# Zero-padded patch matrices for the depthwise convolutions, and layer norms cut into four slices

## The reference, cut to what matters

```
x = mamba_layer(x)                                    # layer 0, a selective scan
g = group_norm(x)                                     # layer 1
x = x + conv1x1(concat(dw3(g), dw5(g), dw7(g))) + b   # three depthwise convolutions
t = tokens(x)                                         # 4 x 4096 tokens of 96 values
for layer in (2, 3):
    t = t + linear_attention(ln(t))                   # no softmax: q (k^T v), 6 heads
    t = t + mlp(ln(t))                                # 96 -> 384 -> 96, values in fp8 e5m2
out = image(t)
ln(v) = (v - mean(v)) / sqrt(var(v) + 1e-5)           # over the 96 values of a token
```

## Time and profile before

| | us |
|---|---|
| median of 3 runs | 4298.84 (4298.52 to 4301.72) |
| the profiled execution, its own time | 4304.14 |
| its span | 4302.3 |
| PE busy | 3678.2 (85%) |
| DVE busy | 3358.8 (78%) |
| POOL busy | 2847.3 (66%) |
| ACT busy | 2386.9 (55%) |
| mean granted clock of TensorE | 0.88 |

### The profile page before, as it was taken

One profiled execution on the slowest core, in us unless ns is written; L12 is line 12 of the kernel. 1 busy time (PEld: TensorE's weight loads), 2 busy tenths in 40 slices (PEclk: granted clock), 3 DMA queues, 4 the chain that ended last, 5 costly groups with the idle time before them and its releaser, 6 DMA issues. The chain is left out here.

```text
span 4302.3 us, 38111 instructions
## 1 busy us (share of the span) xinstructions
PE 3678.2 (85%) x10080; PEld 1484.1 (34%) x10080; DVE 3358.8 (78%) x3987; ACT 2386.9 (55%) x4025; POOL 2847.3 (66%) x2326
## 2 busy tenths in 40 slices
PE   6999899999999999999999999998349987585666
PEld 2333333333333333333333333332113325363554
DVE  4999999999999999999999999999710005646565
ACT  5667666667666666766666766665221112424335
POOL 4988999998899998899998889998300000303113
PEclk8999999999999999999999999999755557676666
DMA  2655555556555565555455555455765564100001
GB/s 86 175 158 161 159 168 156 160 174 166 156 169 156 161 171 159 160 155 161 157 161 163 160 152 165 150 156 159 169 169 163 163 159 110 30 15 15 15 1 30
DMA packets 281726, 588.59 MB, mean 137 GB/s; under 512 B 65847, under 2 KB 135098, under 8 KB 280358
## 3 DMA queue, kind: packets, MB, share of 16 engines
q1 hardware_dynamic: 214438, 516.93, 40.8%
q10 hardware_dynamic: 67072, 69.23, 6.2%
HBM read 532.16 MB, written 58.28 MB: 137 GB/s over the span
## 5 line engine op out<-in xcount | busy, mean ns | idle before, releaser
L796 POOL TENSOR_TENSOR prod<-states,c_rows 128x512 f32<-128x512 f32 x1536 | 1920.4, 1270 | 182.6 <-DVE states L726 148.9
L726 DVE TENSOR_TENSOR_SCAN states<-decay,carry,bpsum 128x512 f32<-128x512 f32 x1344 | 1676.7, 1259 | 0.0
L455 PE MATMUL ypsum<-prod,identity 128*128 128x512 f32 x3072 | 1599.8, 604 | 0.5 <-POOL prod L796 0.3
L561 ACT ACTIVATE decay<-delta,decay_rate 128x512 f32<-128x512 f32 x1344 | 934.7, 711 | 312.1 <-DVE states L726 307.7
L706 DVE TENSOR_TENSOR bpsum<-bpsum,dx 128x512 f32<-128x512 f32 x1344 | 904.4, 673 | 139.8 <-PE bpsum L448 125.4
L1641 POOL TENSOR_TENSOR y<-y,b 128x384 f16<-128x384 f16 x64 | 60.9, 951 | 1054.4 <-ACT y L1458 1054.3
L455 PEld LDWEIGHTS ypsum<-prod,identity 128*128 128x128 f32 x3072 | 583.7, 194 | 433.1 <-issue 285.9
L448 PE MATMUL bpsum<-b_rows,select 96*128 96x512 bf16 x1344 | 521.9, 389 | 209.7 <-DVE states L726 206.4
L448 PEld LDWEIGHTS bpsum<-b_rows,select 96*128 96x128 bf16 x1344 | 129.8, 97 | 960.6 <-DVE states L726 670.6
L1048 PE MATMUL convp<-image,patch_w 88*96 88x512 f32 x384 | 328.0, 1057 | 44.4 <-DMA image<-normed_map 44.4
L561 ACT ACTIVATE bpsum<-delta,decay_rate 128x512 f32<-128x512 f32 x192 | 132.6, 691 | 309.3 <-DVE states L726 308.5
(11 more groups left out here) (188 smaller groups left out, 4538.3 us busy)
## 6 DMA issues: line engine op xcount, KB each, us to landing
c_rows<-bc_map SPq DMA_DIRECT2D x512, 512.0 KB, 3.8
c_rows<-bc_map SPq DMA_DIRECT2D x512, 256.0 KB, 4.0
b_wide<-bc_map ACTq DMA_DIRECT2D x128, 256.0 KB, 4.5
image<-normed_map SPq DMA_DIRECT2D x192, 96.1 KB
depthwise_map<-dw_sums ACTq DMA_DIRECT2D x96, 192.0 KB, 2.7
dw_parts<-depthwise_map SPq DMA_DIRECT2D x16, 1152.0 KB, 7.5
b_wide<-bc_map ACTq DMA_DIRECT2D x128, 128.0 KB, 4.3
normed_map<-padded SPq DMA_DIRECT2D x8, 1155.0 KB, 13.8
```

Source lines behind the costliest of these rows:

```text
L455: pe.matmul(ypsum[:, group % Y_BANKS, :], identity[:, :], prod[:, n % P_RING, :], start=s == 0, stop=s == STATES - 1).then_inc(summed, 1)
L561: act.activation(into, delta[k % 2][:, g, :], ACT.Exp, scale=decay_rate[:, ORDER[k][0], g, s:s + 1]).then_inc(done, 1)
L726: dve.tensor_tensor_scan(states[:, n % H_RING, :], by, add, carry[:, at, u:u + 1], ALU.mult, ALU.add).then_inc(scanned, 1)
L796: pool.tensor_tensor(prod[:, n % P_RING, :], states[:, n % H_RING, :], c_rows[:, n // C_STATES % C_RING, n % C_STATES, :], ALU.mult).then_ ...
```

## The change

It does two things.

The tiles `patch_w` and `image` are made 128 partitions tall, and a patch matrix 128 columns wide. POOL clears both whole before the first load, behind its memsets of `padded`; `zeroed` now comes after the last, and SP waits for it ahead of the first patch loads. The loads go into rows 0 to 87 and columns 0 to 95. Each matmul is of 128 inputs and 128 outputs into all of the bank; ACT still copies 96 rows out. A patch load now has elements of 96 floats (384 bytes), 8 to a partition, where one element had 3072 bytes.

The layer norms are cut into four slices of 8 tiles. Every step takes a slice number k, and its semaphores count slices. In attention DVE makes the four slices of center, add_input where due, the four of variance, the Gram steps, and then one slice of scale after each of the additions 1, 3, 5 and 7; ACT makes one slice of squares after each of the copies 1, 3, 5 and 7, and the four of roots at the end. In MLP the steps of slice k come after the chunks k (center), k + 1 (squares), k + 2 (variance), k + 3 (roots) and k + 4 (scale). Ahead of phase 0 the slices stand between the `add_input`s. A slice of center waits only for its own quarter of the residual, and PE waits before the transposes of a chunk for the slice that it reads.

```diff
-SQUARE_AFTER, ROOT_AFTER = (5, 3), 5
-CENTER_AFTER, VARIANCE_AFTER, SCALE_AFTER = 1, 4, 6
+SLICES = 4
+ATT_SQUARE, ATT_SCALE = (1, 3, 5, 7), (1, 3, 5, 7)
+MLP_CENTER, MLP_SQUARE, MLP_VARIANCE, MLP_ROOT, MLP_SCALE = range(5)
...
-            patch_w = tmp("patch_w", [PATCH, W_RING, W_CHANNELS, 2, PATCH_OUT])
-            image = tmp("image", [PATCH, I_RING, BATCH * ROW_BLOCKS, HALF_ROW])
+            patch_w = tmp("patch_w", [128, W_RING, W_CHANNELS, 2, 128])
+            image = tmp("image", [128, I_RING, BATCH * ROW_BLOCKS, HALF_ROW])
...
-                        sp.dma_start(patch_w[:, j % W_RING, :, :, :].rearrange("p c t m -> p (c t m)"),
+                        sp.dma_start(patch_w[0:PATCH, j % W_RING, :, :, 0:PATCH_OUT].rearrange("p c t m -> p (c t) m"),
                                      dram["patch_rows"][:, W_CHANNELS * j:W_CHANNELS * (j + 1), :, :]
-                                     .rearrange("p c t m -> p (c t m)")).then_inc(patch_loaded[j % W_RING], 16)
+                                     .rearrange("p c t m -> p (c t) m")).then_inc(patch_loaded[j % W_RING], 16)
...
+                    sp.wait_ge(zeroed, 1)
                     for j in range(W_RING):
                         load_patches(j)
...
-                            last = pe.matmul(banks[0:PATCH_OUT, c % 4, :].rearrange("m (n i) -> m n i", i=HALF_SIDE),
+                            last = pe.matmul(banks[:, c % 4, :].rearrange("m (n i) -> m n i", i=HALF_SIDE),
...
                     for i in range(2):
-                        last = pool.memset(padded[:, i, :, :, :, :].rearrange("c f r n i -> c (f r n i)"), 0.0)
-                    last.then_inc(zeroed, 1)
+                        pool.memset(padded[:, i, :, :, :, :].rearrange("c f r n i -> c (f r n i)"), 0.0)
+                    pool.memset(patch_w[:, :, :, :, :].rearrange("p j c t m -> p (j c t m)"), 0.0)
+                    pool.memset(image[:, :, :, :].rearrange("p c n i -> p (c n i)"), 0.0).then_inc(zeroed, 1)
...
                 def turn(p, c, kind, rows):
 
                     fill = fills[kind, p, c]
+                    pe.wait_ge(ln_ready, SLICES * p + c * SLICES // CHUNKS + 1)
...
-                def squares(v):
-
-                    act.wait_ge(ln_centered, v + 1)
-                    act.activation(haug[:, v % 2, :, 0:C], dev[:, :, :], ACT.Square).then_inc(ln_squared, 1)
+                def squares(v, k):
+
+                    act.wait_ge(ln_centered, SLICES * v + k + 1)
+                    tiles = slice(SLICE * k, SLICE * (k + 1))
+                    act.activation(haug[:, v % 2, tiles, 0:C], dev[:, tiles, :], ACT.Square).then_inc(ln_squared, 1)
...
-                        if p + 1 < PHASES and c == SQUARE_AFTER[0]:
-                            squares(p + 1)
+                        if p + 1 < PHASES:
+                            for k in due(ATT_SQUARE, c):
+                                squares(p + 1, k)
                     if p + 1 < PHASES:
-                        roots(p + 1)
+                        for k in range(SLICES):
+                            roots(p + 1, k)
...
                     if layer == 0 and not is_mlp:
-                        dve.wait_ge(rows_taken, CONV_GROUPS * (b + 1))
+                        dve.wait_ge(rows_taken, CONV_GROUPS * b + k + 1)
                     elif not is_mlp:
-                        dve.wait_ge(t_step, CHUNKS * (nth(v - 2) + 1))
+                        dve.wait_ge(t_step, CHUNKS * nth(v - 2) + CHUNKS // SLICES * (k + 1))
                     else:
-                        dve.wait_ge(t_taken, fills[ATT_O, v - 2, CHUNKS - 1] + 1)
+                        dve.wait_ge(t_taken, fills[ATT_O, v - 2, CHUNKS // SLICES * (k + 1) - 1] + 1)
...
                     dve.tensor_tensor(gram[:, 0, 0:C], mp[0:C + 1, 0, 0:C], bff[:, layer, :], ALU.add).then_inc(gram_step, 1)
-                    if p + 1 < PHASES:
-                        scale(p + 1)
...
                                           src[:, tiles, :].rearrange("p j c -> p (j c)"), ALU.add).then_inc(t_taken, 1)
+                        if p + 1 < PHASES:
+                            for k in due(ATT_SCALE, c):
+                                scale(p + 1, k)
...
-                            if c == CENTER_AFTER:
-                                center(p + 1)
-                            if c == VARIANCE_AFTER:
-                                variance(p + 1)
-                            if c == SCALE_AFTER:
-                                scale(p + 1)
+                            if 0 <= c - MLP_CENTER < SLICES:
+                                center(p + 1, c - MLP_CENTER)
+                            if 0 <= c - MLP_VARIANCE < SLICES:
+                                variance(p + 1, c - MLP_VARIANCE)
+                            if 0 <= c - MLP_SCALE < SLICES:
+                                scale(p + 1, c - MLP_SCALE)
...
-                for i in range(CONV_GROUPS):
-                    add_input(i)
-                center(0)
-                add_input(CONV_GROUPS)
-                variance(0)
-                add_input(CONV_GROUPS + 1)
-                scale(0)
-                for i in range(CONV_GROUPS + 2, 2 * CONV_GROUPS):
-                    add_input(i)
+                for i in range(2 * CONV_GROUPS + 1):
+                    if i < 2 * CONV_GROUPS:
+                        add_input(i)
+                    if 0 <= i - 2 < SLICES:
+                        center(0, i - 2)
+                    if 0 <= i - 4 < SLICES:
+                        variance(0, i - 4)
+                    if 0 <= i - 5 < SLICES:
+                        scale(0, i - 5)
```

More of the change, by code:

```diff
@@ L1413, in _, with roots @@
             def _(act):
-                def squares(v):
-                    act.wait_ge(ln_centered, v + 1)
-                    act.activation(haug[:, v % 2, :, 0:C], dev[:, :, :], ACT.Square).then_inc(ln_squared, 1)
-                def roots(v):
-                    act.wait_ge(ln_var, v + 1)
-                    act.activation(stat[:, 2, :], stat[:, 1, :], ACT.Sqrt).then_inc(ln_root, 1)
+                def squares(v, k):
+                    act.wait_ge(ln_centered, SLICES * v + k + 1)
+                    tiles = slice(SLICE * k, SLICE * (k + 1))
+                    act.activation(haug[:, v % 2, tiles, 0:C], dev[:, tiles, :], ACT.Square).then_inc(ln_squared, 1)
+                def roots(v, k):
+                    act.wait_ge(ln_var, SLICES * v + k + 1)
+                    tiles = slice(SLICE * k, SLICE * (k + 1))
+                    act.activation(stat[:, 2, tiles], stat[:, 1, tiles], ACT.Sqrt).then_inc(ln_root, 1)
                 def rows(i):
@@ L1472, in mlp @@
                             add_up(c - 1)
[L1473 to L1476, removed]
+                        if p + 1 < PHASES:
+                            if 0 <= c - MLP_SQUARE < SLICES:
+                                squares(p + 1, c - MLP_SQUARE)
+                            if 0 <= c - MLP_ROOT < SLICES:
+                                roots(p + 1, c - MLP_ROOT)
                     add_up(CHUNKS - 1)
@@ L1487, in _ @@
                 first = 2 * CONV_GROUPS
-                for i in range(CONV_GROUPS):
+                for i in range(first):
                     rows(i)
[L1490 to L1493, removed]
+                    if 0 <= i - 3 < SLICES:
+                        squares(0, i - 3)
+                    if 0 <= i - 4 < SLICES:
+                        roots(0, i - 4)
                 for p in range(PHASES):
@@ L1514, in chain, with center @@
                     dve.wait_ge(dve_step, count[0])
-                def center(v):
+                def center(v, k):
                     b, layer, is_mlp = phase_of(v)
-                    src = residual_of(v)
+                    tiles = slice(SLICE * k, SLICE * (k + 1))
+                    src = residual_of(v)[:, tiles, :]
                     if layer == 0 and not is_mlp:
-                        dve.wait_ge(rows_taken, CONV_GROUPS * (b + 1))
+                        dve.wait_ge(rows_taken, CONV_GROUPS * b + k + 1)
@@ L1529, in center @@
+                    chain(dve.tensor_reduce(stat[:, 0, tiles], src, AXIS.X, ALU.add))
+                    chain(dve.tensor_scalar(stat[:, 0, tiles], stat[:, 0, tiles], 1.0 / C, None, ALU.mult))
+                    dve.tensor_tensor(dev[:, tiles, :], src, stat[:, 0, tiles].unsqueeze(2).to_broadcast([128, SLICE, C]),
                                       ALU.subtract).then_inc(ln_centered, 1)
[L1531 to L1542, removed]
+                def variance(v, k):
+                    tiles = slice(SLICE * k, SLICE * (k + 1))
+                    dve.wait_ge(ln_squared, SLICES * v + k + 1)
+                    chain(dve.tensor_reduce(stat[:, 1, tiles], haug[:, v % 2, tiles, 0:C], AXIS.X, ALU.add))
+                    dve.tensor_scalar(stat[:, 1, tiles], stat[:, 1, tiles], 1.0 / C, LN_EPS, ALU.mult, ALU.add).then_inc(ln_var, 1)
@@ L1544, in add_input, with scale @@
+                def scale(v, k):
```

(20 more changed lines are left out.)

7 lines of the change are left out of this document (2 added, 5 removed).

## The result

The changed kernel takes 4153.6 us (median of 4 runs, 4152.97 to 4156.2), against 4300.1 us before: a ratio of 0.966 (95% interval 0.9644 to 0.9677), 146.5 us less. The forecast was 4147, within 4108 to 4215.

What follows compares the result with a forecast made beforehand. It took the convolution, with PE busy at half clock, as the bound, and DMA as the next limit. Gains of 134 (convolution), 10 (before phase 0) and 14 (attention) less 6 (MLP) make 152: 4298.8 to 4147 us, range 4108 to 4215.

Steps and rivals of the forecast that it cites:

- The clock: Convolution: padded 128x128 matmuls run at clock 1.00 instead of 0.50, bringing PE's time to 167 us.
- Rival B: Convolution: the clock stays at 0.50 despite padding and only the norms count, 4281 us; chance 0.08.
- The convolution's other limit: Convolution: 183 us of DMA work at 94% busy sets the length, 195 us from 328.7, minus 134.
- Small pieces: Convolution: patch loads in 384-byte pieces add 12 us of DMA work, between 9 and 36.
- Before phase 0: Fusing stretch ahead of phase 0: slices between the additions let the last fuse start earlier, gain 10 us.
- Attention: Attention phases: sliced norms gain 2.0 us each, 16 over eight, 14 without the first, which is counted elsewhere.
- an earlier Gram copy: Attention phase: the Gram copy no longer waits behind whole squares and variance, gain 2.0 us a phase.
- MLP: Seven MLP phases with a norm: slices' fixed cost outweighs the idle time saved, loss 0.8 us each, 6 in all.
- Rival A: Convolution: DMA holds it at 240 us through small pieces and queue order, total 4192 us; chance 0.15.
- C: Convolution: transfers hide and PE sets the pace at 167 us, some output chunks keep the clock, 4114 us; chance 0.12.
- D: Norms: the slices' fixed cost lies bare while the clock stays low, slower at 4331 us; chance 0.02.

Runs made afterwards that it cites:

- 88x128: The changed kernel with the convolution's matmuls cut to 88 inputs and 128 outputs; 4268.9 us.
- 96x96: The changed kernel with the convolution's matmuls cut to 96 inputs and 96 outputs, patch loads again in 3072-byte elements; 4154.7 us.

## Why the prediction was right, and where two terms missed

The total came out 6.6 us under the measured 4153.6, which is closer than its terms are: that is luck. The convolution fell by 15 us less than forecast and the stages behind it by 14 more, and the two nearly cancel (152 us forecast, 150.4 between the profiled executions). The rest of the 6.6 comes from taking the 152 off the median of three runs, 4298.8, where the profiled execution before had 4304.1 and the one after stands at its median.

- **The clock** rose as said: 0.50 over 328 us before, 1.00 some 4 us after the first matmul now. The ground, that the new stream has the shape of the scan's, was enough for the forecast but left open which side counts: only the inputs do (88x128 stays at 0.50, 96x96 does not). The page "TensorE: Matmul & The Clock Gate" of the Trainium skill (Part 1) has sustained activity release the throttle; the 88x96 stream, without a pause for 328 us at 0.50, contradicts it as it stands. Rival B, that something which padding doesn't touch holds the clock, is refuted.
- **The convolution's other limit** is the step that was mis-sized: 209.4 us for 195, and what was put as its cause was wrong. "183 us of DMA work at 94%" does not hold. The work is 165 us, and 89% of DMA goes with a stage of 173.6. Nor was 94% a ceiling: it is the mean over a stage with its start and end, and the earlier trace rows, inside that stage, already show 1.04. What costs is what the prediction named and then didn't price by itself: four pauses behind the `x0` stores of 3.1 to 4.9 us (15.7 together), with half clock behind them, which costs 1.7 us after the first and about 3 after each other one (24 matmuls take 12.25, 13.46, 13.58 and 13.58 us there, for some 10.5 at full clock), and smaller pauses, one every four channels, as the patch loads come. Together the pauses are 26.6 us, and PE's busy time is 19 us above its 164 (182.8): some 13 of that are matmuls at the lower clock, the start's 2 among them, and I leave the rest to the ends of the many short groups, which the profile counts in (169.7 busy in the stage of 173.6, at clock 0.99). The two kernels with cut stores and with a deep ring show it.
- **Small pieces** were priced at 12 us of engine time (9 to 36). The runs show 2 to 6 us of engine time, and with the other limits gone some 4 us of the stage at most: even the low end was too high. By "DMA: Bandwidth & Descriptors" of the Trainium skill (Specifications) transfers under 512 bytes are off line rate; the doubling that I assumed from it, an estimate, would have made the term 22, and these loads are far from that.
- **Before phase 0** 10 us were forecast. From the first fusing matmul to the first transposes it was 67.9 us and is 57.6: 10.3.
- **Attention.** From the first Gram product to the last output product the eight phases have 259.1 us before and 238.6 after, 20.5 less; I had 14 for seven of them. Phase 0 has none of it (32.8 before, 33.3 after), so the seven gained 21. The term that was named, an earlier Gram copy, is 1.8 us in the phase shown, for 2.0 forecast. Two smaller ones were left out: the output product follows the Gram copy at 3.93 us for 4.26, since the first small product comes before the clock has fallen (1.00 in that microsecond, 0.50 before), and the output chunks take 14.6 us for 15.4, of which 0.4 is a wait for DVE, busy with the scale, that is gone.
- **MLP.** In the two phases without fusing (43.4 and 43.1 us before) it is 44.0 each, a loss of 0.6 to 0.9 as forecast. The four phases with fusing lose nothing: from their first transposes to their last product they take 42.9 to 43.1 us before and 43.1 after. In the same way all eight MLP phases together have 331.0 us before and 331.5 after, where I had 6 more. Why the loss stays out of the others was not tried. Between the phases, where the fusing products lie, another 3.7 us went (95.6 to 91.9), and the tail behind the last MLP product is 2 us longer; neither was in the forecast.
- **Rival A** (240 us) and **C** (167 us) were both off for the changed kernel; C is nearly what the deep ring and the cut stores together make of it (173.6 and 169.9). **D** did not come: with the clock low and the norms sliced, the kernel is 28 us faster and not slower.

## What to carry to other kernels

A stream of matmuls that is fully busy and yet at the lower clock may have too few inputs: look for a long window with PE at 100% and clock 0.50, and try padding the contraction, the inputs that are summed over, with zero rows (here from 88 to 96 was enough, and columns gave nothing). When a stage gets faster, look at its rings before its bandwidth: each ring's lead in time shrinks with the stage, so a large transfer that was hidden behind 10 us of lead (three channels of 3.4 us) shows behind 5. Forecast a stage by what each queue holds in front of what, and not by the sum of the engines' work alone: a pause of PE costs its own length and then the low clock behind it. Cut work into slices where slices can be spread; in a row they only add their fixed cost.

## What was not expected of the hardware

- In this stream the granted clock depends on the inputs of the matmul: 88x96 and 88x128 at 0.50 for 328 us without a pause, 128x128 and 96x96 at 1.00 some 4 and 6 us after the start, with the same data.
- A pause of 3 to 5 us cost another 1.7 to 3 us behind it, since the clock had fallen: 0.77 over the 6 us after the first, where it costs least.
- Eight times the pieces in the patch loads, of 384 bytes in place of 3072, and with them twice the packets of q1, took only 2 to 6 us more of its time (99 us for 97, 90 for 84).
